# One quadrant of w1 turned by VectorE instead of TensorE, and six sums moved from VectorE to GpSimd

## The reference

```python
def _L0_cond_ref(x, labeler_index, W, lora_A, lora_B_w):
    low = jnp.einsum('bsi,bir->bsr', x, lora_A[labeler_index])           # rank 32
    return jnp.einsum('bsi,oi->bso', x, W) + jnp.einsum('bsr,or->bso', low, lora_B_w) * 0.5

def _L1_cond_ref(x, adapter_mapping, W, b, lora_As, lora_Bs):
    h = jnp.einsum('bti,bir->btr', x, lora_As[adapter_mapping])          # rank 16
    return jnp.einsum('bti,oi->bto', x, W) + b + jnp.einsum('btr,bro->bto', h, lora_Bs[adapter_mapping]) * 2

x = x + _L0_cond_ref(x, itok_B_0_2, L0_W, L0_lora_A, L0_lora_B_w)
x = x + _L1_cond_ref(x, itok_B_0_23, L1_W, L1_b, L1_lora_As, L1_lora_Bs)
```

## Time and profile before

| | us |
|---|---|
| median of 3 runs | 294.84 (294.36 to 294.86) |
| the profiled execution | 294.32 |
| its span, first to last instruction | 292.6 |
| PE busy | 288.8 (99%) |
| DVE busy | 242.8 (83%) |
| ACT busy | 153.9 (53%) |
| POOL busy | 30.4 (10%) |

### The profile page before, as it was taken

One profiled execution on the slowest core, in us unless ns is written; L12 is line 12 of the kernel. 1 busy time (PEld: TensorE's weight loads), 2 busy tenths in 40 slices (PEclk: granted clock), 3 DMA queues, 4 the chain that ended last, 5 costly groups with the idle time before them and its releaser, 6 DMA issues.

```text
span 292.6 us, 4450 instructions
## 1 busy us (share of the span) xinstructions
PE 288.8 (99%) x1337; PEld 236.0 (81%) x1337; DVE 242.8 (83%) x368; ACT 153.9 (53%) x270; POOL 30.4 (10%) x81
## 2 busy tenths in 40 slices
PE   8999999999999999999999999999999999999996
PEld 6888888888888888878878878878878878878885
DVE  3789996999999999999996897797798698695432
ACT  3685576879257537464453463373364355355120
POOL 1718100010000501000100100100100100100000
DMA  6999420800006600093268076068068159013004
GB/s 203 323 322 325 51 37 10 137 1 2 0 0 110 98 27 1 5 148 136 46 100 217 22 130 188 18 103 220 3 108 214 16 103 237 0 36 145 0 1 146
DMA packets 100803, 29.17 MB, mean 100 GB/s; under 512 B 85548, under 2 KB 93996, under 8 KB 100788
## 3 DMA queue, kind: packets, MB, share of 16 engines
q1 hardware_dynamic: 100788, 28.99, 42.7%
HBM read 20.59 MB, written 8.39 MB: 99 GB/s over the span
## 4 chain that ended last, share of the span: by engine, by line
PE 99%; ACT 0%; DVE 0%; issue 0%
PE bank L1204 94%; PE bank L1228 3%; PE bank L1450 1%; PE bank L1416 0%; ACT b_hi L468 0%; DVE y L718 0%
## 5 line engine op out<-in xcount | busy, mean ns | idle before, releaser
L1204 PE MATMUL bank<-v_hi,lhs 128*128 128x512 f32 (+1 forms) x136 | 42.5, 377 | 0.0
L1204 PE MATMUL bank<-vt_hi,s_hi 128*128 128x512 f32 x96 | 37.3, 389 | 0.0
L1204 PE MATMUL bank<-vt_lo,s_hi 128*128 128x512 f32 x96 | 37.3, 389 | 0.0
L1204 PE MATMUL bank<-vt_hi,s_lo 128*128 128x512 f32 x96 | 37.3, 389 | 0.0
L969 DVE STREAM_TRANSPOSE xt<-raw 128x512 int32<-128x512 int32 x32 | 32.4, 1076 | 1.4 <-DMA raw<-in_x 1.4
L1204 PEld LDWEIGHTS bank<-v_hi,lhs 128*128 128x128 f32 x136 | 25.1, 188 | 4.5
L468 ACT ACTIVATE lhs<-xt 128x512 fp32r<-128x512 f32 x32 | 19.6, 626 | 13.0 <-PE bank L1204 12.7
L1204 PE MATMUL bank<-v_lo,lhs 128*128 128x512 f32 (+1 forms) x68 | 25.7, 378 | 0.0
L1204 PE MATMUL bank<-vt_hi,lhs 128*128 128x512 f32 x64 | 22.1, 406 | 0.0
L718 DVE TENSOR_TENSOR lhs<-xt,lhs 128x512 fp32r<-128x512 f32 x32 | 21.7, 686 | 0.3
L434 POOL CAST ac<-c_hi 128x128 fp32r (+1 forms) x16 | 7.2, 450 | 135.5 <-PE bank L1204 98.5
(11 more groups left out here) (167 smaller groups left out, 662.6 us busy)
## 6 DMA issues: line engine op xcount, KB each, us to landing
raw<-in_x SPq DMA_DIRECT2D x32, 256.0 KB, 4.9
out<-y SPq DMA_DIRECT2D x31, 256.0 KB, 2.7
n<-in_L_cond_W SPq DMA_DIRECT2D x16, 256.0 KB, 5.3
a<-in_L_cond_W SPq DMA_DIRECT2D x16, 256.0 KB, 5.2
a_raw<-in_L_cond_lora_A SPq DMA_DIRECT2D x8, 128.0 KB, 2.4
b_raw<-in_L_cond_lora_Bs SPq DMA_DIRECT2D x16, 64.0 KB, 2.1
e_raw<-in_L_cond_lora_Bs SPq DMA_DIRECT2D x32, 32.0 KB, 1.8
a_raw<-in_L_cond_lora_As SPq DMA_DIRECT2D x8, 64.0 KB, 2.4
```

The source lines that it names most:

```text
L1204: return nc.tensor.matmul(ps, lhsT, rhs, start=start, stop=stop, skip_group_check=more)
```

## The change

TensorE no longer turns w1's quadrant 21: its 16 transposes (four turns) go. The quadrant is loaded in another layout, 32 rows to each group of 32 partitions, by 16 DMAs of 64 KB in runs of 32 elements (128 bytes) instead of 4 DMAs of 256 KB in runs of 512 bytes, so that 32x32 blocks turned by VectorE (4 instructions of 128x512, into the SBUF tile `b21`) give the transposed quadrant. `b21_hi` is then made from `b21` in SBUF, and ScalarE's four copies of `b21` out of PSUM go. The a1 gathers are issued ahead of A12's loads. The sums S1, T4 and S4 (two halves each, 128x1024) move from VectorE's queue to GpSimd's. TensorE does `c_first(0, A11)` ahead of B21's adapter part. On ScalarE, `a1_hi` moves behind `b21_hi(1)`, and the second adapter half goes ahead of `s4_hi`. The warm-up stays.

```diff
-    n21 = at("n21", [P, HK, HK, P], F32, 20 * SLOT)
+    n21 = at("n21", [P, HK, H // 32, 32], F32, 20 * SLOT)
@@ SyncE
+            w1_21 = w1[0:H, H:D].rearrange("(nb sl) (j g r) -> j g sl nb r", sl=32, g=GR, r=32)
             for j in range(HK):
-                load_n(n21, 0, 1, j, n21_in[j])
-            for j in range(HK):
-                load_a(a12, 0, 1, j, a12_in[j])
+                for g in range(GR):
+                    sp.dma_start(n21[32 * g:32 * g + 32, j, :, :], w1_21[j, g]).then_inc(n21_in, 16)
...  (the eight a1 gathers)
+            for j in range(HK):
+                load_a(a12, 0, 1, j, a12_in[j])
@@ GpSimd
-            for j in range(HK):
-                pool.wait_ge(a22_in[j // 2], 32)
-                add_eye_a(a22, j, w0_eyed)
+            for h in range(2):
+                for j in range(2 * h, 2 * h + 2):
+                    pool.wait_ge(a22_in[h], 32)
+                    add_eye_a(a22, j, w0_eyed)
+                pool.wait_ge(w0_eyed, HK + 2 * h + 2)
+                pool.wait_ge(s3_made, h + 1)
+                tt(s1[:, PAIR[h], :], a21[:, PAIR[h], :], a22[:, PAIR[h], :], ALU.add, s1_made)
...  (the masks)
+            for h in range(2):
+                pool.wait_ge(t2_made, h + 1)
+                pool.wait_ge(w1_lo_made, HK + 2 * h + 2)
+                tt(t4[:, PAIR[h], :], b21[:, PAIR[h], :], t2[:, PAIR[h], :], ALU.subtract, t4_made)
+            for h in range(2):
+                pool.wait_ge(s2_made, h + 1)
+                pool.wait_ge(w0_lo_made, HK + 2 * h + 2)
+                tt(s4[:, PAIR[h], :], s2[:, PAIR[h], :], a12[:, PAIR[h], :], ALU.subtract, s4_made)
@@ ScalarE
-            act.wait_ge(a1_in, 16 * B)
-            copy(a1_hi ...)
             for j in range(HK):
-                act.wait_ge(turned, T21_AT[j] + 1)
-                bank_copy(b21_hi, j, TURN_BANK[T21_AT[j]], w1_hi_made)
-                bank_copy(b21, j, TURN_BANK[T21_AT[j]], w1_made)
+                if j == 2:
+                    act.wait_ge(a1_in, 16 * B)
+                    copy(a1_hi ...)
+                act.wait_ge(w1_made, 2 * HK + j + 1)
+                high(b21_hi, b21, j, w1_hi_made)
...  (q_half(1) and p_high(1) now stand ahead of the two s4_hi)
@@ VectorE
                 t2_sum(h)
-                s1_sum(h)
                 s2_sum(h)
                 t2_low(h)
                 s2_low(h)
+            dve.wait_ge(n21_in, 64 * HK)
+            dve.wait_ge(v_done, M7 + HK)
+            for j in range(HK):
+                nc.vector.transpose(b21[:, j, :].bitcast(I32),
+                                    n21[:, j, :, :].rearrange("p nb r -> p (nb r)").bitcast(I32)).then_inc(w1_made, 1)
...  (a1_lo, then b21_low(0..3), now SBUF less SBUF, a1d, a12_low(0..3), q_half(0), b22_low(0..1);
...   t4_sum and s4_sum are gone, p_low(1) stands ahead of the two s4_low)
@@ TensorE
                     by_halves(h, S2, T2, m, v_done)
-                    if h == 1 and m == 2:
-                        turn_b21(HK - 1)
-                if h == 0:
-                    for j in range(HK - 1):
-                        turn_b21(j)
+            pe.wait_ge(a1_lo_made, 1)
+            pe.wait_ge(t1_made, HK)
+            pe.wait_ge(w1_made, 2 * HK)
+            c_first(0, A11)
             for j in range(HK):
                 pe.wait_ge(w1_lo_made, HK + j + 1)
                 last = q_step(Q_BANK[0], HK + j, B21, j, False, j == HK - 1)
             last.then_inc(q_done, 1)
-            pe.wait_ge(a1_lo_made, 1)
-            pe.wait_ge(w1_made, 3 * HK)
-            c_first(0, A11)
```

More of the change, by code:

```diff
@@ L160, in two_layer_lora_kernel @@
         n11_in = [sem(f"n11_in{j}") for j in range(HK)]
-        n21_in = [sem(f"n21_in{j}") for j in range(HK)]
+        n21_in = sem("n21_in")
         n22_in = [sem(f"n22_in{j}") for j in range(2)]
@@ L235, in two_layer_lora_kernel @@
         HIGH = [bank[5], bank[4], bank[7], bank[6]]
-        TURN_BANK = [bank[n] for n in (6, 7, 4, 5, 6, 7, 4, 5, 6, 7, 4, 6, 7, 4, 6, 7)]
-        TURNED_THERE = {4: 0, 5: 1, 6: 2, 7: 3, 8: 4, 9: 5, 10: 6, 11: 8, 12: 9, 13: 10, 14: 11, 15: 12}
+        TURN_BANK = [bank[n] for n in (6, 7, 4, 5, 6, 7, 4, 5, 6, 7, 4, 6)]
+        TURNED_THERE = {4: 0, 5: 1, 6: 2, 7: 3, 8: 4, 9: 5, 10: 6, 11: 8}
         Q_BANK = [bank[5], bank[6]]
@@ L539, in _ @@
             s2_t2_high(1)
-            act.wait_ge(a1_in, 16 * B)
-            copy(a1_hi[:, :, :], a1_raw[:, :, :, :].rearrange("p t b r -> p t (b r)"), a1_hi_made, LORA1_SCALE)
             for j in range(HK):
-                act.wait_ge(turned, T21_AT[j] + 1)
-                bank_copy(b21_hi, j, TURN_BANK[T21_AT[j]], w1_hi_made)
-                bank_copy(b21, j, TURN_BANK[T21_AT[j]], w1_made)
+                if j == 2:
+                    act.wait_ge(a1_in, 16 * B)
+                    copy(a1_hi[:, :, :], a1_raw[:, :, :, :].rearrange("p t b r -> p t (b r)"), a1_hi_made, LORA1_SCALE)
+                act.wait_ge(w1_made, 2 * HK + j + 1)
+                high(b21_hi, b21, j, w1_hi_made)
             act.wait_ge(v_done, M6 + HK)
@@ L572, in _ @@
             copy(q_part[:, 0:G1], B0A1_BANK[64:96, 0:G1], b0a1_part_made, LORA0_SCALE)
+            act.wait_ge(b0a1_all_made, 2)
+            q_half(1)
+            p_high(1)
             act.wait_ge(vs_lo_made, S2_AT + 2)
@@ L815, in s3_sum @@
                 tt(s3[:, PAIR[h], :], a21[:, PAIR[h], :], a11[:, PAIR[h], :], ALU.subtract, s3_made)
-            def s1_sum(h):
-                dve.wait_ge(w0_eyed, HK + 2 * h + 2)
-                dve.wait_ge(s3_made, h + 1)
-                tt(s1[:, PAIR[h], :], a21[:, PAIR[h], :], a22[:, PAIR[h], :], ALU.add, s1_made)
             def t2_sum(h):
@@ L895, in _, with b21_low @@
                                            op1=ALU.subtract).then_inc(a1_lo_made, 1)
-            tt(a1d[:, :, :], raw_a1[:, HK:KT, :], raw_a1[:, 0:HK, :], ALU.subtract, a1d_made)
-            def b21_low(j):
-                dve.wait_ge(w1_made, 2 * HK + j + 1)
-                tt(b21_lo[:, j, :], TURN_BANK[T21_AT[j]][:, :], b21_hi[:, j, :].bitcast(F32), ALU.subtract, w1_lo_made)
-            b21_low(0)
-            b21_low(1)
-            t4_sum(0)
-            b21_low(2)
-            b21_low(3)
+            def b21_low(j):
+                dve.wait_ge(w1_hi_made, HK + j + 1)
+                dve.wait_ge(w1_made, 2 * HK + j + 1)
+                low(b21_lo, b21, b21_hi, j, w1_lo_made)
+            for j in range(HK):
+                b21_low(j)
+            tt(a1d[:, :, :], raw_a1[:, HK:KT, :], raw_a1[:, 0:HK, :], ALU.subtract, a1d_made)
             for j in range(HK):
@@ L913, in _ @@
             b22_low(1)
-            s4_sum(0)
-            s4_sum(1)
             p_low(0)
@@ L930, in _ @@
             q_half(1)
+            p_low(1)
             for h in range(2):
```

21 lines of the change are left out of this document (2 added, 19 removed).

## The result

The changed kernel takes 304.75 us (median of 4 runs, 303.82 to 305.48) where the kernel before takes 294.74 in the same series (294.36 to 294.86): a ratio of 1.034, 95% interval 1.030 to 1.038. The profiled execution took 303.82 us, its span is 302.1, TensorE's mean granted clock 0.989. The forecast was 303.5, with a range from 294.6 to 307.5.

What follows compares the result with a forecast made beforehand. TensorE was taken to bound the kernel, with VectorE little ahead. Waits of 9.2 and 0.2 less 1.75 gave +7.7 us, plus 1.0 for the clock: 303.0 profiled, 303.5 median, range 294.6 to 307.5.

Steps and rivals of the forecast that it cites:

- GpSimd holds VectorE for 2.2 us a sum: Each 128x1024 sum on GpSimd locks the shared SBUF port, making VectorE's two-SBUF-input instructions wait up to 2.2 us.
- S1 half 0 and M7: S1's first half holds VectorE from 23.85 to 26.05, so `s3_low(1)` reaches TensorE's product 0.1 us late.
- S2 times T2: S1's second half delays VectorE's `s2_low`; TensorE starts this product's halves 1.7 and 0.4 us late.
- Transposes: VectorE's four turns of quadrant 21, estimated from x's rows at 0.97 us each, run from 41.6 to 45.5.
- The long wait: Three GpSimd sums ahead of the fourth `a12_low` make TensorE wait 7 us, starting `c_first(1, A12)` at 59.1, not 51.55.
- The clock: TensorE's 7 us idle stretch may lower its clock afterwards; taken as 1.0 us out of 0 to 1.9.
- The loads: Quadrant 21's short-run loads end by 31, a1's gathers go out about 28 to 39; no cost in the forecast case.
- Behind it the rest is in time.: After `c_first(1, A12)`, `b22_low` and `s4_low` end before TensorE wants them, so no further waiting is added.
- A microsecond taken from TensorE's queue is a microsecond of the time.: TensorE, busy 99% of the span, sets the time if operands are ready; removing the turns gives 1.75 us.
- 0.2 in `q_step`: TensorE's `q_step`, ahead of `c_first(1, A12)`, waits 0.2 us for VectorE's `b21_low(3)`.
- free sums: Rival: GpSimd's long sums hardly hold VectorE, so all 1.75 us come and the time is 293.1; chance 0.15.
- The one in which VectorE keeps the lock: Rival: GpSimd gets in only at gaps or beside PSUM reads; +1.3 us, 296.2, from 294.8 to 298; chance 0.14.

Runs made afterwards that it cites:

- the idle adds: Changed kernel with S1, T4 and S4 back on VectorE, plus six GpSimd adds of 128x1024 whose results nobody reads: 307.87 us, ratio 1.0453.
- the filled wait: Changed kernel with 44 matmuls of a constant, result unread, put on TensorE just ahead of its wait before `c_first(1, A12)`: 303.20 us, ratio 1.0279.
- the kernel with the order alone: Kernel before, with only Q's second half copy and p's high and low parts moved ahead of S4's on ScalarE and VectorE: 296.15 us, ratio 1.0051.
- the old order: Changed kernel with all six sums back on VectorE and S4's parts again ahead of Q's second half copy and p's parts: 298.62 us, ratio 1.0134.
- the best order tried: Kernel with six sums and S4's order back, plus quadrant 21's first low part and both T4 sums moved into VectorE's idle time: 296.34 us, ratio 1.0055.
- the kernel with S1 back: Changed kernel with only S1's two halves back on VectorE, T4 and S4 staying on GpSimd: 304.04 us, ratio 1.0305.

## Why the prediction was right, and where it was not

By the steps of the prediction:

- **GpSimd holds VectorE for 2.2 us a sum.** Right, and partly by luck: the figure came from a difference of 0.27 us between two rows of different instructions, scaled up by eight. Undisturbed, the first of the six took 2.40 (forecast 2.35), and three of the idle adds took 2.20 to 2.27. The six stretched neighbours are those named, with 1.95 to 2.22 us more each.
- **S1 half 0 and M7.** The forecast had TensorE 0.1 late; it was 0.72. GpSimd's sum started at 24.25, not at 23.85, since quadrant 22 came 0.85 us later in this execution. That arrival is a term which the sum held fixed and which varies by up to 3 us.
- **S2 times T2.** 1.7 and 0.4 late were forecast, 36.1 and 42.0 as starts; it was 1.47 and 0.38, at 36.28 and 42.23.
- **Transposes.** Forecast 0.97 each, measured 0.59 to 0.60 from start to start. The estimate was taken from x's rows, which read and write in another order. With this term right and the rest unchanged, `c_first(1, A12)` would have come out at 57.6.
- **The long wait.** Forecast 7.0 us and 59.1, measured 5.92 and 58.28, released by `a_lo`, as told. Three sums lie ahead of the fourth `a_low`. The shorter transposes take 1.5 off; the later start, 0.47 us of waiting for a1's high part and the sums' 2.2 us plus handovers give part of it back, and the fourth `a_lo` ends at 58.23 against 58.8. The forecast had added 0.3 from there to TensorE's start, where 0.05 was measured, and had TensorE ready 0.25 earlier than it was.
- **The clock.** Forecast 1.0 out of 0 to 1.9, measured 1.6 on TensorE itself in the trace, and 1.2 to 1.55 at the end by the filled wait.
- **The loads.** The sixteen issues took 12.75 us from 18.87, as forecast. The gathers went out from 32.64 to 41.51 and not from 28 to 39; a start at 28 does not fit the prediction's own 31 for the end of the issues. In this execution ScalarE did not wait for them; in the traces of two later kernels it did, 1.65 and 1.89 us, a price that the prediction put at nothing.
- **"Behind it the rest is in time."** Wrong, and the one step whose reasoning failed and not only its size. It holds for the two operands it names: `b22_low` ended at 61.09 and `s4_low` at 74.09, and TensorE waited for neither. But TensorE starts 0.85 us late for `u_st` at 133.64. The earlier trace rows was read up to 50 us only, where VectorE is 0.9 to 1.5 us ahead; from 64 us on it has almost no lead: in its profiled execution the kernel with the order alone has VectorE 2.1 us late at the first `v` and ends 2.1 late. VectorE's lag is 6.72 us when it copies Q (58.15 against 51.43) and 9.54 at its first `v`. The 2.82 between are 2.08 for p's low part beside S4's second sum, 1.22 + 1.35 + 0.40 of idle time (the last two from the new order, which the prediction put at nothing; the first is the clock's way to the end), less 2.27 for the two sums of S4 which it no longer does (2.78, within 0.04).
- **"A microsecond taken from TensorE's queue is a microsecond of the time."** Half of it. The earlier trace rows says what the chain that ended last ran over, not what else is full. With the turns gone and the sums back the kernel is slower than before, by 1.3% with the old order and 0.55% with the best order tried.

So the forecast was close partly by cancelling: 1.1 us too much in the long wait and 0.2 in `q_step`, where nothing waited, against 0.4 too little for the first three late starts together, 0.6 for the clock, 0.85 for `u_st` and 0.3 of small change. That is 0.8 in all, the profiled execution's 303.82 against 303.0 (the prediction's own two sums, 7.65 and 7.55 where it writes 7.7, leave 0.1 open); and the median lies 0.93 above it where 0.5 had been taken.

The rivals: free sums are refuted by the idle adds. The one in which VectorE keeps the lock is refuted for the five sums that got in at the next handover, but it describes the sixth: S4's second half asked at 58.37 and ended at 63.34, after two `b_lo` rows of 1.20 us had gone ahead of it. The kernel with S1 back shows the same (4.95 us from 59.49), the one with the wait filled too (4.98 from 59.02), and the idle add at 59.05 took 6.81, with four VectorE instructions of two SBUF inputs ahead of it. It recurs at the same place; a first use of an instruction does not explain it, since five like it had gone before. What decides it is left open: a series of small adds at many points of VectorE's queue would have shown it and wasn't run.

## What to carry to other kernels

An idle GpSimd is no free helper of a VectorE whose instructions have two SBUF inputs: an add of 1024 elements saves VectorE 1.13 us and stops it for 2.2. Before work is taken off the engine that the chain names, read the lead of the engine that feeds it over the whole span, not just around the change, by the last point where the feeder idles; here VectorE's first `v` at 64 us gave the time of eleven kernels out of fourteen to within 0.5 us. And an instruction moved within a full queue should go where that queue idles: three of them were worth 2.3 us.

## What the hardware showed that was not expected

- GpSimd's clear of 128x1024 (0.95 to 0.97 us) leaves a VectorE instruction with two SBUF inputs at its length (four `a_lo` in 2.49), where two adds took the same four to 5.88. The prediction had read the clear in the earlier trace rows as a lock held to its end; for instructions with two SBUF inputs that is wrong, and why that small instruction took 1.14 us is open.
- A waiting GpSimd instruction was passed over at two handovers or more at one place, in four kernels (4.95, 4.97, 4.98, 6.81 us).
- A turn of 128x512 in fp32 took 0.68 us with plain addresses (0.60 from start to start), against the 1.08 of the earlier trace rows; one of 128x32 took 0.18 (0.10 from start to start).
- The landing of loads asked for in the same order varied from one execution to the next: the first add on w0's quadrant 22 started anywhere from 22.4 to 25.5 us in fourteen traces, and this moved the start of the transposes by more than 1 us. Two single traces are compared only after taking this off.
- After idle stretches the granted clock fell to 0.50 (5.9 us of idle time) and, after 2.0 us near 128, to 0.66 over the next 5 us in some runs and not in others of the same kernel.
